# Routed tiles in pairs, three product buffers, a ring of twelve gathered tiles, and scatters in column halves

## The chip, the cores and the metric

The kernel runs on one core of a Trainium2 chip. The metric is device time in microseconds (us) of one execution. Engines are named as in the profile: PE (TensorE, with its weight loads apart as PEld), DVE (VectorE), ACT (ScalarE), POOL (GpSimd, which also issues the indirect DMAs) and SP (SyncE, which issues the plain ones). SBUF is the on-chip memory, PSUM the memory into which PE writes, in 8 banks of 512 fp32 columns for each of 128 partitions.

## The reference

The input is 64 sequences of 64 tokens with 256 columns, 4096 tokens. Each sequence has a category (0 to 15) and a language (0 to 3). Three steps run one after the other, the first two only feed the third:

```python
x = x + attn(x @ cond_weight[category] + cond_bias[category])   # 16 heads of 16, linear position bias
x = x @ A[language].T @ B[language].T + lang_embed[language]    # rank 16
def geglu(h): a, g = split(h, 2); return a * gelu(g)
ys = geglu(x @ Ws1 + bs1) @ Ws2 + bs2                           # shared expert, 512 hidden
w  = softmax over the two largest of (x @ Wr + br) / 1.5        # 2 of 12 experts per token
yr = sum_e w[:, e] * (geglu(x @ We1[e] + be1[e]) @ We2[e] + be2[e])   # 768 hidden each
out = residual stream + ys + yr
```

The experts of a token are known only on the chip. Each of the 4096 tokens has two, so there are 8192 pairs of a token and an expert. They are sorted by expert into tiles of 128 rows, each tile of one expert; rounded up for every expert this is at most 75 tiles, and the kernel always runs 75 (rows that belong to no token point at a zero row, and their results are added to spare rows behind the output).

## The kernel before

The first 412 us or so do attention, the low-rank step, the router and most of the shared expert; the change leaves them alone but for the stores. The routed stage that follows takes the rest. Its input rows are short: because the language step has rank 16, a token is kept as 69 numbers (64 low-rank ones, the language and a one; the router's gate stands in a 70th, rows are 72 wide) in `gated_rows` in HBM, and the first expert layer has been multiplied beforehand with the low-rank matrices (`w1m`, a 64-row matrix for every expert, and `w1b` for the biases and language rows).

One routed tile t goes through these steps. Tiles are numbered 0 to 74; s is t modulo the ring `RING` = 6, and buffers alternate by s modulo 2.

- POOL `load_rows` (L496): an indirect DMA gathers 128 rows of 288 bytes into `s_row[s]`, one of six buffers.
- ACT `widen` (L700, L702): two copies bring the rows into the form that can be transposed.
- PE `rows_transpose` (L1543, L1544): two transposes into PSUM bank 7. DVE `rowT_copy` (L1117, L1119) takes them out.
- The tile's expert weights are copied from `w1m` and `w1b` to a fixed place by `copy_first`, a third each by ACT, DVE and POOL (all on L270), and the bias rows by POOL (L511). Each such copy first loads the expert's number into a register (L269).
- PE `first_layer` (L1556, L1562): for each of three column blocks two bf16 matmuls for the biases and four for the rows, which the trace shows as eight fp32 records; two 64-row matmuls run beside each other. Output in banks 0 to 3, one set for all tiles.
- ACT `gelus` (L708), two halves; DVE `multiply` (L1127), two halves, into `actT_sb`, two buffers.
- PE `second_layer` (L1575): six matmuls of 256 columns, twelve records, into bank 4 or 5.
- DVE `gate_bias` (L1134) scales the expert's second bias row by the gate; `add_bias` (L1143) multiplies the product by the gate, adds it, and writes `y_sb`, one of three buffers.
- POOL `add_rows` (L504): an indirect DMA adds the 128 rows of 1024 bytes to the rows of the output. Two tiles can hold rows of one token, so a scatter waits (`d_add`) until the one before has landed.

The order on every engine is written by hand. PE runs first_layer(t+1), rows_transpose(t+2), second_layer(t). DVE runs rowT_copy(t+1), both halves of multiply(t), the weight copy for t+2, gate_bias(t), add_bias(t-1). POOL runs the copies for t+2, add_rows(t-1) and load_rows(t+5). Engines hand over through semaphores (`rowT_ps`, `rowT_sb`, `h_ps`, `g_ok`, `act_ok`, `y_ps`, `y_ok`), each of which is raised once or twice per tile.

Before the first scatter the residual plus shared result must stand in the output: SP `store_out` (L371) stores 32 tiles of it from `x2res`.

## Time and profile before

| | us |
|---|---|
| median of 3 runs | 805.79 (805.69 to 806.53) |
| profiled execution, its own time | 806.17 |
| its span, first to last instruction | 804.4 |
| granted TensorE clock, mean over the span | 0.996 |

The span is what the profile's rows cover; 1.8 us of the profiled execution lie outside it. Columns of a line of instruction groups: line, engine, operation, output <- inputs, count | busy time in us, mean ns of one | idle time of the engine before them, and who ended it. The first routed matmul starts at 434.4 us, the first scatter at 445.9, the last at 797.5. Matmuls are pipelined, so a row's length on PE is longer than the distance to the next; distances between starts tell the pace.

### The profile page before, as it was taken

The numbers are of one execution on the slowest core, as the hardware profiler recorded it, in microseconds if no ns is written. First come the engines' busy times: TensorE is split into PE (matmuls) and PEld (weight loads), VectorE is DVE, ScalarE is ACT, GpSimd is POOL, SyncE is SP. The second block draws the span as 40 slices with busy tenths as digits, with TensorE's granted clock in tenths as the row PEclk, the third lists the DMA queues.
The fourth block names the chain that finished last, engine by engine and source line by source line (L and its number), as shares of the span: only waits on it lengthen the run. The fifth ranks groups of instructions, "written<-read, shape, count | busy, mean of one in ns | idle before, by whom it ended". The sixth has DMA issues, their size and how long they took to land.

```text
span 804.4 us, 27682 instructions
## 1 busy us (share of the span) xinstructions
PE 783.6 (97%) x9379; PEld 658.2 (82%) x9380; DVE 575.9 (72%) x1350; ACT 294.3 (37%) x883; POOL 405.4 (50%) x511
## 2 busy tenths in 40 slices
PE   7999999999999999999999999999999999999994
PEld 6788888888888888777778888888888888888883
DVE  2999877777777777679884676666666666666661
ACT  1444444444444444542222333333333333333330
POOL 3133244444444444401012777777777777777762
PEclk9999999999999999999999999999999999999998
DMA  9553355555565554048734233223222322232222
GB/s 277 153 187 101 112 170 180 182 174 177 180 182 181 182 182 146 2 158 232 231 130 139 28 42 37 33 35 39 35 34 33 38 38 33 34 40 36 33 31 26
DMA packets 49325, 86.11 MB, mean 107 GB/s; under 512 B 7298, under 2 KB 27970, under 8 KB 49122
## 3 DMA queue, kind: packets, MB, share of 16 engines
q1 hardware_dynamic: 33778, 68.83, 27.2%
q0 software_dynamic: 13888, 15.13, 14.3%
q10 hardware_dynamic: 1584, 1.10, 0.5%
q8 instruction: 54, 0.88, 0.5%
q14 instruction: 21, 0.17, 0.1%
HBM read 68.48 MB, written 16.55 MB: 106 GB/s over the span
## 4 chain that ended last, share of the span: by engine, by line
PE 90%; DVE 5%; issue 2%; DMA 1%; SPq 0%; POOL 0%; ACT 0%; DVEq 0%
PE ps L1575 24%; PE ps L1562 13%; PE ps L1234 7%; PE ps L1473 6%; PE ps L1332 4%; PE ps L1556 4%; PE ps L1306 3%; PE ps L1250 3%; PE ps L1279 3%; PE ps L1462 3%; PE ps L1219 3%; PE ps L1543 2%; PE ps L1339 2%; PE ps L1292 2%; PE ps L1321 2%
## 5 line engine op out<-in xcount | busy, mean ns | idle before, releaser
L1575 PE MATMUL ps<-arena,stage 128*128 x900 | 206.6, 379 | 0.0
L1575 PEld LDWEIGHTS ps<-arena,stage 128*128 128x128 f32 x900 | 165.2, 190 | 19.5
L504 POOL DMA_INDIRECT out_dram<-stage,to_row x75 | 120.6, 1609 | 76.0 <-DVE stage L1143 71.3
L708 ACT ACTIVATE stage<-ps 128x384 f32<-128x384 f32 x150 | 65.4, 488 | 241.6 <-PE ps L1562 241.6
L1562 PE MATMUL ps<-token_rows,token_rows_T 64*128 64x128 f32 x1800 | 129.2, 272 | 0.0
L1562 PEld LDWEIGHTS ps<-token_rows,token_rows_T 64*128 64x128 f32 x1800 | 118.8, 188 | 1.7
L496 POOL DMA_INDIRECT token_rows<-gated_rows,from_row x75 | 75.1, 1001 | 61.6 <-DVE to_row L1022 38.9
L1117 DVE COPY token_rows<-ps 128x128 f32<-128x128 f32 x75 | 21.9, 292 | 111.8 <-PE ps L1544 111.8
L408 POOL TENSOR_TENSOR arena<-arena 128x256 f32<-128x256 f32 x32 | 23.4, 732 | 139.3 <-DVE arena L832 132.3
L1127 DVE TENSOR_TENSOR stage<-ps,stage 128x384 f32<-128x384 f32 x150 | 76.0, 549 | 1.8 <-ACT stage L708 1.8
L795 DVE TENSOR_REDUCE arena<-ps 128x8 f32<-128x512 f32 x64 | 43.9, 686 | 42.4 <-PE ps L1270 42.0
L1234 PE MATMUL ps<-arena 128*128 128x128 f32 x512 | 63.1, 276 | 0.9 <-ACT arena L565 0.8
L1556 PE MATMUL ps<-token_rows,token_rows_T 64*128 64x256 bf16 x450 | 62.1, 273 | 0.0
L1234 PEld LDWEIGHTS ps<-arena 128*128 128x128 f32 x512 | 59.7, 192 | 1.6 <-ACT arena L565 1.0
L1473 PE MATMUL ps<-ws,stage 128*128 128x256 f32 x256 | 59.1, 384 | 0.0
L578 ACT ACTIVATE arena<-arena 128x512 f32<-128x512 f32 x64 | 40.3, 630 | 50.0 <-DVE arena L797 49.7
L1473 PEld LDWEIGHTS ps<-ws,stage 128*128 128x128 f32 x256 | 47.4, 190 | 9.8 <-issue 4.0
L797 DVE TENSOR_TENSOR arena<-ps,arena 128x512 f32<-128x512 f32 x64 | 44.3, 691 | 2.2
L270 DVE COPY token_rows_T<-w_merged 128x256 f32 x75 | 44.7, 596 | 0.7 <-issue 0.7
L1119 DVE TENSOR_SCALAR token_rows<-ps,consts 128x128 bf16<-128x128 f32 x150 | 45.1, 343 | 0.0
L511 POOL COPY token_rows_T<-w_bias 128x384 bf16 x75 | 42.8, 570 | 0.9 <-issue 0.8
L590 ACT COPY arena<-arena 128x128 f32<-128x128 f32 x64 | 15.9, 295 | 73.4 <-DVE arena L817 73.4
(173 smaller groups left out, 1473.8 us busy)
## 6 DMA issues: line engine op xcount, KB each, us to landing
stage<-in_we_dram SPq DMA_DIRECT2D x36, 512.0 KB, 4.7
arena<-in_cond_w_dram SPq DMA_DIRECT2D x64, 256.0 KB, 2.8
arena<-in_we_dram SPq DMA_DIRECT2D x12, 768.0 KB, 6.0
arena<-in_x_both_dram SPq DMA_DIRECT2D x31, 256.0 KB, 2.7
arena<-in_L_cond_bias_dram SPq DMA_DIRECT2D x64, 64.0 KB, 2.9
out_dram<-arena SPq DMA_DIRECT2D x32, 128.0 KB, 2.7
be_bc<-in_be_rows_dram SPq DMA_DIRECT2D x13, 192.0 KB, 3.4
gated_rows<-token_rows POOLq DMA_DIRECT2D x2, 1152.0 KB, 11.6
```

The costliest lines, as they stand in the source:

```text
L270: copy(w1x[s % 2][:, j * CW:(j + 1) * CW], w1m[:, ds(e * (NJ * CW) + j * CW, CW)]).then_inc(w1x_ok[j], 1)
L496: pool.indirect_dma_start(s_row[s], None, gated_rows, bass.IndirectOffsetOnAxis(from_row[:, t:t + 1], 0)).then_inc(d_row[s], 16)
L504: pool.indirect_dma_start(out_rows, bass.IndirectOffsetOnAxis(to_row[:, t:t + 1], 0), y_sb[t % YR], None, compute_op=ALU.add).then_inc(d_a ...
L708: nc.scalar.activation(g_sb[hf].rearrange("p (j n) -> p j n", n=P), first_out[1][:, :, hf, :], ACT.Gelu).then_inc(g_ok, 1)
L797: V.tensor_tensor(probs[:, 512 * half:512 * half + 512].rearrange("p (g h k) -> p g h k", g=2, k=S), scores[:, banks], top.unsqueeze(3).to ...
L1119: last = V.tensor_scalar(s_langT[s % 2][:, hf * P:(hf + 1) * P], ps[:, 7, P:2 * P], col["half"][:, hf:hf + 1], None, ALU.mult)
L1127: V.tensor_tensor(actT_sb[s % 2][:, hf, :].rearrange("p (j n) -> p j n", n=P), first_out[0][:, :, hf, :], g_sb[hf].rearrange("p (j n) -> p ...
L1234: last = mm(ps[:, bank, at + m * P:at + (m + 1) * P], wm[w][:, k, m * P:(m + 1) * P], cT[:, k, :], start=(k == 0), stop=(k == KC - 1))
L1473: last = mm(ps[:, 4 + v, half * D:(half + 1) * D], sh_aT[half][:, k, v * P:(v + 1) * P], ws2[:, k, :], start=(k == 0), stop=(k == HS // P ...
L1556: mm(first_out[g][:, j].rearrange("p h n -> p (h n)"), w1bx[s % 2].bitcast(bf16)[64 * g:64 * g + 64, at], s_langT[s % 2][64 * g:64 * g + 6 ...
L1562: last = mm(first_out[g][:, j, hf, :], w1x[s % 2][64 * g:64 * g + 64, j * CW + hf * P:j * CW + (hf + 1) * P], s_rowT[s % 2][64 * g:64 * g ...
L1575: last = mm(ps[:, 4 + s % 2, 0:D], actT_sb[s % 2][:, hf, j * P:(j + 1) * P], arena[:, ds(e * E2 + (NJ * hf + j) * D, D)], start=(hf == 0 a ...
```

## The change

1. PSUM is divided anew. The first layer's output gets two sets, one for odd and one for even tiles, in banks 0 to 5 (each set is one and a half banks for each of its two parts, so both sets share two banks). The second layer's output goes to bank 6 for odd tiles and bank 7 for even ones; transposes share bank 7.
2. Tiles are handled in pairs (`two_tiles`): PE does the first layers of t and t+1, the transposes of t+2 and t+3, then the second layers of t-2 and t-1. DVE and ACT follow in an order of their own.
3. `actT_sb` gets a third buffer, in the space of `ws2`, which the shared expert has done with.
4. POOL makes no weight copies any more. DVE copies two thirds of `w1m`, ACT one third and the bias rows.
5. The ring of gathered rows has twelve places.
6. The output is two tensors of 128 columns. Each tile is scattered by two indirect DMAs of 128 rows of 512 bytes, each half waiting for the same half of the tile before; stores are two per tile as well, and the halves are joined on the host.
7. The last unit of the shared expert gets PSUM of its own (`last_shared`), so that the routed tiles can begin beside it.

On POOL, in the routed stage, this stands before for one tile (a scatter, a gather, two copies with their register loads) and then the next tile's scatter:

```order
L504 DMA out_dram<-stage,to_row 4224x256 [waits d_dummy,d_add,y_ok]
L496 DMA token_rows<-gated_rows,from_row 128x72
L269 TENSOR_LOAD expert_of [waits h_ps]
L269 ISA x2
L270 ISA
L270 COPY token_rows_T<-w_merged 128x256
L510 TENSOR_LOAD expert_of
L510 ISA x2
L511 ISA
L511 COPY token_rows_T<-w_bias 128x384
L504 DMA out_dram<-stage,to_row 4224x256 [waits d_dummy,d_add,y_ok]
```

and this now for two tiles (L513 is a half of a scatter, L503 a gather):

```order
L513 DMA out_dram<-stage,to_row 4224x128 [waits d_add0,d_dummy,y_ok]
L513 DMA out_dram<-stage,to_row 4224x128 [waits d_add1]
L503 DMA token_rows<-gated_rows,from_row 128x72 [waits y_ok] x2
L513 DMA out_dram<-stage,to_row 4224x128 [waits d_add0,d_dummy,y_ok]
L513 DMA out_dram<-stage,to_row 4224x128 [waits d_add1]
```

The copies are gone, the scatters have doubled, and both gathers of a pair stand between the scatters of an odd and an even tile, while those of an even and the next odd tile follow each other directly.

On VectorE, the loop before, one tile (waits of the copies of transposed rows, then multiply, weight copy, scaling, add):

```order
L1117 COPY token_rows<-ps 128x128 [waits rowT_ps]
L1119 TENSOR_SCALAR token_rows<-ps,consts 128x128 x2
L1124 ISA
L1127 TENSOR_TENSOR stage<-ps,stage 128x384 [waits g_ok]
L1124 REGISTER_ALU
L1127 TENSOR_TENSOR stage<-ps,stage 128x384 [waits g_ok]
L269 ISA
L269 TENSOR_LOAD expert_of
L269 ISA x2
L270 ISA
L270 COPY token_rows_T<-w_merged 128x256
```

and now the piece of the pair between the second copy of transposed rows and the add of the pair's first product (L275 copies weights, L1171 scales the bias):

```order
L1148 TENSOR_SCALAR token_rows<-ps,consts 128x128 x2
L274 ISA
L274 TENSOR_LOAD expert_of
L274 ISA x2
L275 ISA
L275 COPY token_rows_T<-w_merged 128x256
L274 TENSOR_LOAD expert_of
L274 ISA x2
L275 ISA
L275 COPY token_rows_T<-w_merged 128x256
L1168 TENSOR_LOAD expert_of
L1168 ISA x2
```

A second such scaling follows, then the add, and only behind it the multiply of the pair's second tile. Four instructions that each need a register load now stand in front of the add.

The core of the diff:

```diff
-RING = 6
+RING = 12
...
+        actT_sb.append(ws2[:, 0:NJ, :].rearrange("p k n -> p (k n)").rearrange("p (h n) -> p h n", h=2))
-        first_out = [ps[:, 2 * g:2 * g + 2, :].rearrange("p b n -> p (b n)")[:, 0:2 * HH].rearrange(
-            "p (j h n) -> p j h n", h=2, n=P) for g in range(2)]
+        hidden_ps = ps[:, 0:6, :].rearrange("p b n -> p (b n)").rearrange(
+            "p (g s j h n) -> p s g j h n", g=2, s=2, h=2, n=P)
+        def first_out(t, s):
+            return hidden_ps[:, 0 if s % 2 == 1 or isinstance(t, int) and t == 0 else 1]
+        last_shared = [ps[:, 6, 0:D], ps[:, 7, 0:D]]
...
             def store_out(n, d_out):
                 sp.wait_ge(comb_ok, n + 1)
-                sp.dma_start(out_rows[ds(n * P, P), :], x2res[:, ds(n * D, D)]).then_inc(d_out, 16)
+                for h in range(2):
+                    sp.dma_start(out_half[h][ds(n * P, P), :], x2res[:, ds(n * D + h * P, P)]).then_inc(d_out, 16)
...
             def add_rows(t, s):
                 pool.wait_ge(y_ok, t + 1)
-                if t > 0:
-                    pool.wait_ge(d_add, 16 * t)
-                pool.wait_ge(d_dummy, 16)
-                pool.indirect_dma_start(out_rows,
-                                        bass.IndirectOffsetOnAxis(to_row[:, t:t + 1], 0),
-                                        y_sb[t % YR], None, compute_op=ALU.add).then_inc(d_add, 16)
-
-            def copy_last(t):
-                copy_first(pool, nc.gpsimd.tensor_copy, t, t, 2)
-                e = pool.value_load(expert_of[0:1, ds(t, 1)], min_val=0, max_val=NE - 1)
-                nc.gpsimd.tensor_copy(w1bx[t % 2].bitcast(bf16), w1b[:, ds(e * (NJ * P), NJ * P)]).then_inc(w1bx_ok, 1)
+                pool.wait_ge(d_dummy, 32)
+                for h in range(2):
+                    part = slice(h * P, (h + 1) * P)
+                    if t > 0:
+                        pool.wait_ge(d_add[h], 16 * t)
+                    pool.indirect_dma_start(out_half[h],
+                                            bass.IndirectOffsetOnAxis(to_row[:, t:t + 1], 0),
+                                            y_sb[t % YR][:, part], None, compute_op=ALU.add).then_inc(d_add[h], 16)
...
+            def next_rows(t):
+                pool.wait_ge(y_ok, t + 1)
+                if t + RING < NS:
+                    load_rows(t + RING, t % RING)
+            for t in range(1, NS, 2):
+                if t > 1:
+                    add_rows(t - 2, (t - 2) % RING)
+                    next_rows(t - 2)
+                    next_rows(t - 1)
+                add_rows(t - 1, (t - 1) % RING)
+                if t == 1:
+                    next_rows(0)
+            for t in (NS - 2, NS - 1):
+                add_rows(t, t % RING)
...
+            def tile_weights(t, s):
+                copy_first(act, copy, t, s, 0)
+                e = act.value_load(expert_of[0:1, ds(t, 1)], min_val=0, max_val=NE - 1)
+                copy(w1bx[s % 2].bitcast(bf16), w1b[:, ds(e * (NJ * P), NJ * P)]).then_inc(w1bx_ok, 1)
+            def two_tiles(t, k, q):
+                for d in range(2):
+                    gelus(t + d, k + d, RING // 2 * q + (k + 1) // 2)
+                    if not (isinstance(t, int) and t + d + 2 >= NS):
+                        tile_weights(t + d + 2, k + d + 2)
+                for d in (4, 5):
+                    if not (isinstance(t, int) and t + d >= NS):
+                        widen(t + d, (k + d) % RING, 16 * q + 16 * ((k + d) // RING) + 16)
...
+            def multiply(t, s):
+                for hf in range(2):
+                    dve.wait_ge(g_ok, 2 * t + (hf + 1))
+                    if hf == 0 and isinstance(t, int) and t < 3:
+                        dve.wait_ge(shy_ps, NT - 2 if t == 0 else NT)
+                    elif hf == 0:
+                        dve.wait_ge(y_ps, t - 2)
+                    V.tensor_tensor(actT_sb[s % 3][:, hf, :].rearrange("p (j n) -> p j n", n=P),
+                                    first_out(t, s)[:, 0, :, hf, :], g_sb[hf].rearrange("p (j n) -> p j n", n=P),
+                                    ALU.mult).then_inc(act_ok, 1)
+            def tile_weights(t, s):
+                for j in (1, 2):
+                    copy_first(dve, V.tensor_copy, t, s, j)
...
             def add_bias(t, s):
+                bank = 6 if s % 2 == 1 or isinstance(t, int) and t == 0 else 7
                 dve.wait_ge(y_ps, t + 1)
                 dve.wait_ge(gb_ok, t + 1)
                 if not (isinstance(t, int) and t < YR):
...
+                    for h in range(2):
+                        dve.wait_ge(d_add[h], 16 * t - 16 * (YR - 1))
+                V.scalar_tensor_tensor(out=y_sb[s % YR], in0=ps[:, bank, 0:D],
                                        scalar=s_row[s][:, W_COL:W_COL + 1], in1=gated_be2[s % 2],
                                        op0=ALU.mult, op1=ALU.add).then_inc(y_ok, 1)
...
+            def two_tiles(t, k):
+                known = isinstance(t, int)
+                multiply(t, k)
+                if not (known and t + 2 >= NS):
+                    for d in (2, 3):
+                        rowT_copy(t + d, (k + d) % RING, t + 4)
+                    tile_weights(t + 2, k)
+                if not (known and t == 1):
+                    gate_bias(t - 2, (k - 2) % RING)
+                gate_bias(t - 1, (k - 1) % RING)
+                if not (known and t == 1):
+                    add_bias(t - 2, (k - 2) % RING)
+                multiply(t + 1, k + 1)
+                if not (known and t + 2 >= NS):
+                    tile_weights(t + 3, k + 1)
+                add_bias(t - 1, (k - 1) % RING)
...
                 last.then_inc(h_ps, 1)
...
+            def second_layer(t, s):
+                e = pe.value_load(expert_of[0:1, ds(t, 1)], min_val=0, max_val=NE - 1)
+                bank = 6 if s % 2 == 1 or isinstance(t, int) and t == 0 else 7
+                if not (isinstance(t, int) and t == 0):
+                    pe.wait_ge(y_ok, max(t - 1, 1) if isinstance(t, int) else t - 1)
+                if bank == 7:
+                    pe.wait_ge(rowT_sb, min(t + 5, NS) if isinstance(t, int) else t + 5)
                 for hf in range(2):
                     pe.wait_ge(act_ok, 2 * t + (hf + 1))
...
                     for j in range(NJ):
...
+                        last = mm(ps[:, bank, 0:D], actT_sb[s % 3][:, hf, j * P:(j + 1) * P],
                                   arena[:, ds(e * E2 + (NJ * hf + j) * D, D)], start=(hf == 0 and j == 0),
                                   stop=(hf == 1 and j == NJ - 1))
                 last.then_inc(y_ps, 1)
...
+            def two_tiles(t, k):
+                known = isinstance(t, int)
+                for d in (0, 1):
+                    first_layer(t + d, k + d)
+                for d in (2, 3):
+                    if not (known and t + d >= NS):
+                        rows_transpose(t + d, (k + d) % RING)
+                for d in (2, 1):
+                    if not (known and t < d):
+                        second_layer(t - d, (k - d) % RING)
```

## Rows read from the trace of the kernel before

**Rows 1.** The page: busy time, share of the span, instructions, by engine.

```profile
PE 783.6 (97%) x9379; PEld 658.2 (82%) x9380; DVE 575.9 (72%) x1350; ACT 294.3 (37%) x883; POOL 405.4 (50%) x511
```

**Rows 2.** Who waited for whom, 460 to 804: us, times, longest.

```profile
ACT stage L708 <- PE ps L1562: 223.0, 70, 3.9
...
POOL out_dram L504 <- DVE stage L1143: 69.2, 71, 3.6
```

**Rows 3.** PE in order of time: start, length, what; one tile.

```profile
600.70 0.38 PE L1575 MATMUL ps<-arena,stage 128*128 x1
601.01 0.28 PE L1556 MATMUL ps<-token_rows,token_rows_T 64*128 64x256 bf16 x2
...
602.78 0.33 PE L1543 MATMUL ps<-consts,token_rows 128*128 128x128 f32 x1
602.95 0.27 PE L1544 MATMUL ps<-consts,token_rows 128*128 128x128 f32 x1
603.06 2.76 PE L1575 MATMUL ps<-arena,stage 128*128 x12
...
605.75 0.28 PE L1556 MATMUL ps<-token_rows,token_rows_T 64*128 64x256 bf16 x2
```

**Rows 4.** VectorE in order of time, and the scatter behind it.

```profile
432.63 0.28 DVE L270 COPY token_rows_T<-w_merged 128x256 f32 x1
433.29 0.29 DVE L270 COPY token_rows_T<-w_merged 128x256 f32 x1 [0.37 <-issue]
...
603.26 0.29 DVE L1117 COPY token_rows<-ps 128x128 f32<-128x128 f32 x1 [1.55 <-PE ps L1544]
...
603.98 1.01 DVE L1127 TENSOR_TENSOR stage<-ps,stage 128x384 f32<-128x384 f32 x2
...
605.95 0.48 DVE L1143 SCALAR_TENSOR_TENSOR stage<-ps,token_rows,token_rows_T 128x256 f32<-128x256 f32 x1
...
606.72 1.61 POOL L504 DMA_INDIRECT out_dram<-stage,to_row  x1 [0.89 <-DVE stage L1143]
...
780.14 0.29 DVE L270 COPY token_rows_T<-w_merged 128x256 f32 x1
780.58 0.35 DVE L1134 TENSOR_SCALAR token_rows_T<-be_bc,token_rows 128x256 f32 x1
```

**Rows 5.** GpSimd: scatters and gathers (groups), and one gather behind a scatter.

```profile
L504 POOL DMA_INDIRECT out_dram<-stage,to_row x75 | 120.6, 1609 | 76.0 <-DVE stage L1143 71.3 <-issue 4.7
L496 POOL DMA_INDIRECT token_rows<-gated_rows,from_row x75 | 75.1, 1001 | 61.6 <-DVE to_row L1022 38.9 <-issue 22.7
...
447.78 1.01 POOL L496 DMA_INDIRECT token_rows<-gated_rows,from_row  x1 [0.31 <-issue]
```

**Rows 6.** GpSimd's two plain DMAs of 128 rows (288 and 1024 bytes).

```profile
L454 POOL DMA_DIRECT2D gated_rows<-be_bc x1 | 0.8, 761 | 0.0
L455 POOL DMA_DIRECT2D out_dram<-be_bc x1 | 0.6, 592 | 0.0
```

**Rows 7.** Scatters: median us to landing; the last two; their landings.

```profile
out_dram<-stage,to_row POOLq DMA_INDIRECT x75, 3.8
...
791.56 1.55 POOL L504 DMA_INDIRECT out_dram<-stage,to_row  x1 [3.00 <-DVE stage L1143]
...
797.53 1.55 POOL L504 DMA_INDIRECT out_dram<-stage,to_row  x1 [4.42 <-issue]
...
DMA to landing us min/median/max: 3.7/4.5/5.2
```

**Rows 8.** Start of the routed stage: tile 1 on PE, and POOL.

```profile
439.99 0.28 PE L1556 MATMUL ps<-token_rows,token_rows_T 64*128 64x256 bf16 x2
...
442.99 0.40 POOL L270 COPY token_rows_T<-w_merged 128x256 f32 x1 [15.44 <-DMA out_dram<-arena]
```

**Rows 9.** A gather and a VectorE copy that began during it.

```profile
623.52 1.00 POOL L496 DMA_INDIRECT token_rows<-gated_rows,from_row  x1 [0.31 <-issue]
...
623.86 0.76 DVE L270 COPY token_rows_T<-w_merged 128x256 f32 x1
```

More of the change, by code:

```diff
@@ L47, in adaln_attn_moe @@
     a = args
-    out_rows = out
     ctx = ExitStack()
@@ L535, in _ @@
+            for t in (NS - 2, NS - 1):
+                add_rows(t, t % RING)
+            for h in range(2):
+                pool.wait_ge(d_add[h], 16 * NS)
         @block.scalar
@@ L722, in _ @@
             act.wait_ge(shx_ok, TOK // U)
+            act.wait_ge(l_cut, 4 * (NE + 1))
             for t in range(2):
@@ L725, in _ @@
             for t in range(2):
-                copy_first(act, copy, t, t, 0)
+                tile_weights(t, t)
             shared_gelu(TOK // U - 1)
-            routed_tiles(0)
-            with act.Fori(1, NS // RING) as q:
-                routed_tiles(q)
-            routed_tiles(NS // RING, last=True)
+            widen(2, 2, 16)
+            gelus(0, 0)
+            tile_weights(2, 2)
+            for t in (3, 4):
+                widen(t, t, 16)
+            for k in range(1, RING, 2):
+                two_tiles(k, k, 0)
+            with act.Fori(1, NS // RING - 1) as q:
+                for k in range(1, RING, 2):
+                    two_tiles(RING * q + k, k, q)
+            for k in range(1, RING, 2):
+                two_tiles(NS - 3 - RING + k, k, NS // RING - 1)
+            two_tiles(NS - 2, 1, NS // RING)
         @block.vector
@@ L1163, in _ @@
             dve.wait_ge(r_done, 1)
             dve.wait_ge(shx_ok, TOK // U)
-            rowT_copy(0, 0)
+            rowT_copy(0, 0, 1)
             for t in range(2):
-                copy_first(dve, V.tensor_copy, t, t, 1)
+                tile_weights(t, t)
             for v in range(2):
                 combine(TOK // U - 2, v, 0)
+            for t in (1, 2):
+                rowT_copy(t, t, 3)
+            multiply(0, 0)
+            tile_weights(2, 2)
+            for v in range(2):
+                combine_last(v)
@@ L1170, in _ @@
             dve.wait_ge(d_be2, 16)
-            routed_tiles(0, first=True)
+            for k in range(1, RING, 2):
+                two_tiles(k, k)
             with dve.Fori(1, NS // RING) as q:
-                routed_tiles(q)
-            routed_tiles(NS // RING, last=True)
-            add_bias(NS - 1, (NS - 1) % RING)
+                for k in range(1, RING, 2):
+                    two_tiles(RING * q + k, k)
+            two_tiles(NS - 2, 1)
+            for t in (NS - 2, NS - 1):
+                gate_bias(t, t % RING)
@@ L1177, in _ @@
+            for t in (NS - 2, NS - 1):
+                add_bias(t, t % RING)
         @block.tensor
```

164 lines of the change are left out of this document (65 added, 99 removed).

## Prediction

> **What bounds the kernel now.** I read the page's busy table first, then who waited for whom over the routed stage (the last 364 us), then one routed tile in order of time on TensorE, VectorE and GpSimd, then the tail. The busy table has PE at 97% [rows 1], and the waits show ACT, DVE and POOL waiting for others while PE itself has no entry to speak of [rows 2]: PE sets the pace. One tile on PE [rows 3]: the first layer starts at 601.01 and the next one at 605.75, a period of 4.74. The second layer starts at 603.06 and its last matmul at 600.70 + 4.74 = 605.44, so eleven steps take 2.38, 0.216 each, twelve 2.60, and the next first layer is 0.09 late. I read that as the change of shape between 128 rows and pairs of 64, and give the same 0.09 to the other change, so the first layer's 601.01 to 602.78 is 1.68 + 0.09. The two transposes take 0.17 and 0.11. POOL is the second: per tile a gather of 1.00 and a scatter of 1.61, both pure issuing work, plus two copies of weights [rows 5]. It still waits for VectorE's result, 69.2 us in 71 times, 1.0 per tile [rows 2], so it has slack, but not much.
>
> **Pairs on PE.** Two first layers, four transposes, two second layers: 3.36 + 0.09 + (0.17 + 3 x 0.11) + 5.20 + 0.09 = 9.24 per pair, against 2 x 4.74 = 9.48. That removes 0.24 in each of 37 pairs, 8.9 us, if nothing else is late. The expert number that PE loads between the two second layers has twelve queued matmuls in front of it; I cost it nothing.
>
> **VectorE and ScalarE.** Counted from a pair's start at 0: the last transpose starts at 3.84, VectorE begins 0.31 later (602.95 to 603.26) at 4.15, copies both gathered rows at 0.72 each (603.26 to 603.98) until 5.59, then two weight copies and two bias scalings, each with an address loaded in front of it. From copy to copy that is 0.66 (432.63 to 433.29), from copy to scaling 0.44 (780.14 to 780.58) [rows 4]; with 0.66, 0.50, 0.50 and 0.35 the product is added at 7.60, done 8.08, and the two multiplies take 1.01 until 9.09. The next pair's first layer waits for the second of them. With a hand-over of 0.29, as from L1143's end (605.95 + 0.48) to the scatter at 606.72, that is 9.38, already a little past PE's 9.24. So even with POOL out of the picture the gain is 37 x 0.1 = 3.7 us rather than 8.9; I keep both ends. VectorE's extra copy (0.28 alone) is in this sum. ScalarE takes over the 128x384 bias copy. It waits for PE 223.0 us in 70 tiles [rows 2], 6.4 per pair, and two more small copies fit in there at anything up to 3 us each: nothing. The third product buffer and the doubled PSUM of the first layer take waits away from nobody who waits today.
>
> **GpSimd.** Here is the term that decides. Per pair it now issues four half scatters and two gathers in order, and nothing else. What does half a scatter cost? The trace has no scatter of 512-byte rows, so I bound it. The gather of 288-byte rows takes 1.00, the scatter of 1024-byte rows 1.61 [rows 5]; were it bytes, a half would lie at 1.19 by a line through the two. But two plain writes of 128 rows show the opposite of growth with bytes, 0.59 for 1024-byte rows and 0.76 for 288-byte rows [rows 6]. A half still has 128 row numbers and 128 additions. I take 1.61, with 1.00 as the lower end (and 0.8, half of it, as the extreme).
>
> The Trainium skill ("DMA: Bandwidth & Descriptors", Anatomy of one DMA, the gpsimd path) says the cost of such a DMA is about 2 us fixed plus its bytes over 436 GB/s, most of the fixed part being the receipt of the last write. By that rule 64 KB saved is an estimated 0.15 us of a transfer, so two halves cost nearly two wholes. It speaks of the whole transfer, not of the issuing; by rows 6 the trace agrees that bytes matter little.
>
> Behind each of these instructions POOL is free again only 0.31 later (447.78, "issue") [rows 5]. So the issuing alone is 4 x 1.61 + 2 x 1.00 + 6 x 0.31 = 10.30 per pair: more than PE's 9.24 and more than today's 9.48.
>
> There is a wait inside it too. A half may be issued only when the same half of the tile before has landed. Landing takes 3.8 from the issue's start in the median, and at the end of the kernel POOL's next scatter started 0.77 after the 5.2 it took there (791.56 + 5.2 = 796.76, start 797.53; of the last two landings I give the longer to tile 73, with the shorter the hand-over would be 2.3) [rows 7]. In POOL's order h0 of an even tile and h0 of the odd tile behind it have only one half scatter between them, 2 x 1.92 = 3.84, but need 3.8 + 0.77 = 4.57. Between odd and even the two gathers fill the time. So POOL's pair is 2 x 1.92 + 2 x 1.31 + 4.57 = 11.03. A half may land sooner than a whole, which brings it back towards 10.30; I take 11.03, since 3.8 already contains 1.61 of issuing and I leave that unchanged. With three y buffers VectorE's add waits for the scatter three tiles back, then PE for VectorE, so the whole pipeline settles at POOL's pace and PE sits idle for about 1.8 per pair.
>
> **The sum.** The first pair's first layers start where tile 1's starts now, at 439.99 [rows 8]; tile 0's second layer starts 3.36 + 0.59 later, its last matmul 2.38 after that, the add 0.51 on (605.44 to 605.95), the scatter 0.77 after the add (605.95 to 606.72) [rows 4]: 447.6. The stores of the shared part become two per tile; POOL waited for them until 442.99 [rows 8] and needs them 4.6 later than that, so nothing. From tile 0's scatter to tile 74's there are 37 pairs. The last gather is of row 74, issued behind tile 62, so 31 of them hold gathers, 31 x 11.03 = 341.9; in the last six POOL needs 2 x 4.57 = 9.14 and PE's 9.24 counts, 55.4. Then the second half starts 1.92 later, and from there to the end I take today's 804.4 - 797.5 = 6.8. Together 447.6 + 341.9 + 55.4 + 1.9 + 6.8 = 853.6, against the span of 804.4. Outside the span lie 806.2 - 804.4 = 1.8; the profiled execution is 0.4 over the median of the runs. Forecast: 853.6 + 1.8 - 0.4 = 855.
>
> **The rivals.**
> - *Half a scatter costs 1.0 or less.* For it: nothing in rows 6 is an indirect DMA, and the gather shows that 128 row numbers can be issued in 1.00. Then POOL needs 2 x 1.31 + 2 x 1.31 + (3.2 + 0.77) = 9.2 and VectorE's chain or PE sets 9.24 to 9.48: the gain of 37 x 0.1 to 0.24 comes through, and about 1.6 in the tail, since h0 lands earlier. Time about 800, between 795 and 805. This is the case on the other side. With s for a half, landing and issuing together make POOL's pair 3s + 6.2, which passes today's 9.48 at s = 1.09: there it decides.
> - *In between, 1.2 to 1.4*, as by bytes. With 1.3: 2 x 1.61 + 2.62 + (3.5 + 0.77) = 10.1, and 31 x 10.1 + 55.4 + 457.7 = 826 (457.7 are the 447.6, 1.9 and 6.8 of the sum, and 1.8 - 0.4).
> - *VectorE is held by POOL's issuing.* The weight copy that started at 623.86, while the gather of 623.52 ran, took 0.76 instead of 0.28 and ended 0.10 after the gather [rows 9]. So a copy between SBUF tiles waits until some 0.18 before the end of a POOL instruction. Today POOL's issuing meets at most one such copy per tile. After the change POOL issues nearly all the time, and four such VectorE instructions stand in the chain in front of the add. If two of them meet a half scatter for up to 1.43 each, the chain is 9.38 + 2.86 = 12.2 and leads (a copy met for less costs less): 31 x 12.2 + 55.4 + 457.7 = 891. Against it: in the chain's window POOL is mostly between its pairs of halves, waiting for landings.
> - *POOL is held by VectorE.* The Trainium skill ("SBUF — State Buffer", Who interferes with whom) says that an exclusive lock goes to whichever of the two starts first and blocks the other entirely. So far the trace shows one direction, VectorE waiting; the gathers stayed at 1.00. As a mechanism here: six VectorE instructions of 0.28 to 0.35 per pair, each delaying POOL by its length, make 11.03 + 1.9 = 12.9 and 31 x 12.9 + 55.4 + 457.7 = 913.
>
> **Chances.** Forecast (a half at 1.5 to 1.65, POOL's pace, 10.3 to 11.3 per pair, so 832 to 862) 0.50; VectorE held 0.16; POOL held 0.05; in between 0.12; a half at 1.0 or less 0.17, of which 0.14 come out faster by more than 0.2% and 0.03 within it. 0.2% (1.6 us) is about what runs of this kernel can tell. Faster 0.14, within 0.17 - 0.14 = 0.03, slower 0.83. The range of 803 to 888 leaves out most of the fast case and most of the last.
>
> **What would show it.** In the profile after: the mean of the scatter row (1.6 with x150 for me, 1.0 for the first rival); POOL's busy share over 80% in the routed slices; PE's busy share falling and PE or VectorE waiting for POOL or for a DMA; a period of 11 us per pair that drops to about 9.2 for the last six; VectorE's weight copies at 0.28 (forecast) or over 1 us (third rival); scatters longer than 1.61 (fourth). I am wrong if the half scatter's mean is under 1.1, or if POOL waits for VectorE every tile as it does now.

## The result and the profile after

The changed kernel takes 844.15 us in the median of four runs (841.85 to 845.8), the kernel before 805.9 on the same chip. The ratio is 1.0474, 95% interval 1.0461 to 1.0488: 38 us slower. The profiled execution took 841.85, with a span of 839.8. The forecast was 855, slower.

The page of the changed kernel: the busy table, the busy row of GpSimd in 40 slices, the scatters' group, the one of VectorE's additions (`add_bias`, from here on simply additions), and the scatters' issues to landing.

```profile
PE 783.3 (93%) x9379; PEld 663.3 (79%) x9380; DVE 571.3 (68%) x1425; ACT 330.5 (39%) x958; POOL 453.6 (54%) x437
...
POOL 3242244444444445010043777877778777878775
...
L513 POOL DMA_INDIRECT out_dram<-stage,to_row x150 | 237.8, 1585 | 79.2 <-issue 53.2
...
L1182 DVE SCALAR_TENSOR_TENSOR stage<-ps,token_rows,token_rows_T 128x256 f32<-128x256 f32 x75 | 36.2, 482 | 78.4 <-DMA out_dram<-stage,to_row 76.3
...
out_dram<-stage,to_row POOLq DMA_INDIRECT x150, 3.3
```

Half a scatter takes GpSimd 1585 ns, a whole one took 1609 [rows 5]. There are 150 now, so scatters take 237.8 us of it instead of 120.6. Landing, the time from the start of the issue to the semaphore event that tells of its end, fell only from 3.8 [rows 7] to 3.3.

Who waited for whom in the changed kernel from 460 us to the end (us, times, longest):

```profile
DVE stage L1182 <- DMA out_dram<-stage,to_row: 76.3, 51, 3.5
POOL out_dram L513 <- issue: 52.9, 137, 1.3
...
PEld ps L1621 <- DVE stage L1159: 19.1, 19, 1.3
...
PE ps L1621 <- DVE stage L1159: 11.6, 17, 0.9
```

In [rows 2] GpSimd waited for VectorE, 69.2 us. Now VectorE waits for scatters to land, 76.3 us, before it may write a product buffer again, and TensorE waits for VectorE. GpSimd's "issue" is 137 times the gap behind an indirect DMA, 0.3 us, or the rest of a landing.

GpSimd in order of time, one pair of the changed kernel and the start of the next:

```profile
627.32 1.56 POOL L513 DMA_INDIRECT out_dram<-stage,to_row  x1 [1.71 <-DMA out_dram<-stage,to_row]
629.18 1.56 POOL L513 DMA_INDIRECT out_dram<-stage,to_row  x1 [0.30 <-issue]
631.05 1.01 POOL L503 DMA_INDIRECT token_rows<-gated_rows,from_row  x1 [0.30 <-issue]
632.37 0.98 POOL L503 DMA_INDIRECT token_rows<-gated_rows,from_row  x1 [0.30 <-issue]
633.66 1.62 POOL L513 DMA_INDIRECT out_dram<-stage,to_row  x1 [0.30 <-issue]
635.59 1.57 POOL L513 DMA_INDIRECT out_dram<-stage,to_row  x1 [0.30 <-issue]
637.69 1.55 POOL L513 DMA_INDIRECT out_dram<-stage,to_row  x1 [0.53 <-issue]
```

I call the two halves of a tile's scatter h0 and h1. From pair to pair here 637.69 - 627.32 = 10.37, and five of its six intervals are one issue plus 0.3. The only longer wait, 0.53, stands before 637.69: h0 of the next tile, 4.03 after the h0 of 633.66. This wait is not always so short: before 627.32 it was 1.71. In the whole stretch with gathers, from 450.75 to 780.69 (the starts of tile 0's and tile 62's first halves), 31 pairs took 329.94, 10.64 each.

TensorE in windows of the changed kernel (PE busy is the first number behind the length):

```profile
446.00:520.00 74.00, 72.54 (x700) 64.05 (x699) 48.83 (x147) 33.37 (x102) 54.28 (x39) 1.00 0.29 31
520.00:780.00 260.00, 235.01 (x2177) 200.65 (x2177) 152.19 (x441) 99.69 (x293) 205.84 (x149) 1.00 0.32 33
780.00:822.00 42.00, 39.52 (x326) 34.03 (x322) 23.38 (x66) 12.70 (x36) 32.90 (x22) 1.00 0.35 33
```

It loses 25 us (260.00 - 235.01) from 520 to 780, at a granted clock of 1.00, so a lower clock has no part in it. In the first 74 us it loses little: the three product buffers let it run ahead.

### The profile page after: what moved, and what is told of

Read it like the earlier page. It is cut to its first block, busy times and chain, and to the rows that moved or that the text cites. A ratio compares the mean times of both kernels' runs of the same rounds, so it can differ in the third digit from the quotient of the medians.

```text
span 839.8 us, 27855 instructions
## 1 busy us (share of the span) xinstructions
PE 783.3 (93%) x9379; PEld 663.3 (79%) x9380; DVE 571.3 (68%) x1425; ACT 330.5 (39%) x958; POOL 453.6 (54%) x437
## 4 chain that ended last, share of the span: by engine, by line
PE 49%; POOL 28%; issue 11%; DVE 6%; DMA 5%; SPq 1%; DVEq 1%; ACT 0%; POOLq 0%
POOL out_dram L513 22%; PE ps L1290 6%; POOL token_rows L503 6%; PE ps L1531 5%; DMA out_dram<-stage,to_row 4%; PE ps L1388 4%; PE ps L1362 3%; PE ps L1306 3%; PE ps L1335 3%; PE ps L1518 3%; PE ps L1275 3%; PE ps L1644 2%; PE ps L1395 2%; PE ps L1348 2%; PE ps L1627 2%
## 5 line engine op out<-in xcount | busy, mean ns | idle before, releaser
L513 POOL DMA_INDIRECT out_dram<-stage,to_row x150 | 237.8, 1585 | 79.2 <-issue 53.2
L1644 PE MATMUL ps<-arena,stage 128*128 x600 | 137.4, 382 | 8.8 <-DVE token_rows L1148 5.8
L1644 PEld LDWEIGHTS ps<-arena,stage 128*128 128x128 f32 x600 | 111.6, 190 | 27.6 <-issue 13.6
L1627 PE MATMUL ps<-token_rows,token_rows_T 64*128 64x128 f32 x1800 | 127.2, 272 | 0.0
L503 POOL DMA_INDIRECT token_rows<-gated_rows,from_row x75 | 74.8, 997 | 63.2 <-DVE to_row L1050 40.6
L1182 DVE SCALAR_TENSOR_TENSOR stage<-ps,token_rows,token_rows_T 128x256 f32<-128x256 f32 x75 | 36.2, 482 | 78.4 <-DMA out_dram<-stage,to_row 76.3
L1644 PE MATMUL ps<-arena,ws 128*128 x300 | 69.8, 382 | 2.3 <-DVE stage L1159 1.8
L1159 DVE TENSOR_TENSOR stage<-ps,stage 128x384 f32<-128x384 f32 x100 | 50.8, 549 | 28.3 <-ACT stage L721 17.3
L1644 PEld LDWEIGHTS ps<-arena,ws 128*128 128x128 f32 x300 | 56.0, 190 | 11.7 <-issue 4.4
L275 DVE COPY token_rows_T<-w_merged 128x256 f32 x150 | 46.6, 331 | 8.9 <-issue 7.5
L1171 DVE TENSOR_SCALAR token_rows_T<-be_bc,token_rows 128x256 f32 x75 | 27.6, 368 | 31.1 <-issue 30.4
L1621 PEld LDWEIGHTS ps<-token_rows,token_rows_T 64*128 64x128 bf16 x450 | 22.8, 96 | 30.0 <-DVE stage L1159 19.1
```

What stands on the lines that cost most here:

```text
L275: copy(w1x[s % 2][:, j * CW:(j + 1) * CW], w1m[:, ds(e * (NJ * CW) + j * CW, CW)]).then_inc(w1x_ok[j], 1)
L503: pool.indirect_dma_start(s_row[s], None, gated_rows, bass.IndirectOffsetOnAxis(from_row[:, t:t + 1], 0)).then_inc(d_row[s], 16)
L513: pool.indirect_dma_start(out_half[h], bass.IndirectOffsetOnAxis(to_row[:, t:t + 1], 0), y_sb[t % YR][:, part], None, compute_op=ALU.add). ...
L1159: V.tensor_tensor(actT_sb[s % 3][:, hf, :].rearrange("p (j n) -> p j n", n=P), first_out(t, s)[:, 0, :, hf, :], g_sb[hf].rearrange("p (j n ...
L1621: mm(first_out(t, s)[:, g, j].rearrange("p h n -> p (h n)"), w1bx[s % 2].bitcast(bf16)[64 * g:64 * g + 64, at], s_langT[s % 2][64 * g:64 * ...
L1627: last = mm(first_out(t, s)[:, g, j, hf, :], w1x[s % 2][64 * g:64 * g + 64, j * CW + hf * P:j * CW + (hf + 1) * P], s_rowT[s % 2][64 * g:6 ...
```

## The experiments

### One scatter of whole rows

The pairs, the ring, the third product buffer and the new order are kept; rows are scattered whole into one output tensor, with the stores and waits that go with it.

```diff
-                for h in range(2):
-                    part = slice(h * P, (h + 1) * P)
-                    if t > 0:
-                        pool.wait_ge(d_add[h], 16 * t)
-                    pool.indirect_dma_start(out_half[h],
-                                            bass.IndirectOffsetOnAxis(to_row[:, t:t + 1], 0),
-                                            y_sb[t % YR][:, part], None, compute_op=ALU.add).then_inc(d_add[h], 16)
...
+                if t > 0:
+                    pool.wait_ge(d_add, 16 * t)
+                pool.indirect_dma_start(out_rows,
+                                        bass.IndirectOffsetOnAxis(to_row[:, t:t + 1], 0),
+                                        y_sb[t % YR], None, compute_op=ALU.add).then_inc(d_add, 16)
```

> The changed kernel with its pairs, its ring of twelve, its three product buffers and its order on every engine, but one scatter of whole rows into one output tensor again. My theory: the doubled scatters are the whole loss. GpSimd then issues 2 x 1.6 for scatters and 2 x 1.0 for gathers, with four gaps of 0.31 that is 6.4 us a pair, and the landing of one scatter before the next costs about 4.1 to 4.6 from scatter to scatter, so two of them take 9.1 at most; TensorE's 9.24 a pair is the bound again. From the first scatter at 450.8: 37 pairs x 9.3 to 9.5 and about 9 at the end give a span of 804 to 811 and a time of 806 to 813 by 37 full pairs; since the first ten pairs ran ahead of the scatters in the changed kernel, I take 798 to 812, thus no clear difference from 805.9. Rival A: pairs, ring and buffers cost by themselves (longer VectorE chain, later start): 825 or more. Rival B: the new order gains much and the halves hid it: below 790.

814.05 us, ratio to the kernel before 1.0099 (1.0082 to 1.0116). Of the 38 us the halves are 30, and 8 are left without them: 2 us above the range I expected, and well under rival A's 825. In the spans (812.3 against 804.4) 5.5 of it are the start, the first scatter at 451.33 instead of 445.8; 1.3 are the 74 steps to the last scatter, 353.0 against 351.7; 1.1 lie behind that. So the question is why the steps gained nothing. GpSimd in order of time, at two places:

```profile
568.51 1.63 POOL L509 DMA_INDIRECT out_dram<-stage,to_row  x1 [0.43 <-issue]
573.16 1.58 POOL L509 DMA_INDIRECT out_dram<-stage,to_row  x1 [3.02 <-DVE stage L1176]
575.04 1.02 POOL L501 DMA_INDIRECT token_rows<-gated_rows,from_row  x1 [0.31 <-issue]
576.36 0.97 POOL L501 DMA_INDIRECT token_rows<-gated_rows,from_row  x1 [0.30 <-issue]
577.88 1.62 POOL L509 DMA_INDIRECT out_dram<-stage,to_row  x1 [0.55 <-issue]
...
795.12 1.55 POOL L509 DMA_INDIRECT out_dram<-stage,to_row  x1 [2.99 <-DVE stage L1176]
799.75 1.55 POOL L509 DMA_INDIRECT out_dram<-stage,to_row  x1 [3.08 <-DMA out_dram<-stage,to_row]
804.30 1.55 POOL L509 DMA_INDIRECT out_dram<-stage,to_row  x1 [3.00 <-DMA out_dram<-stage,to_row]
```

From start to start it is 4.65, 4.72, 4.63, 4.55, whether gathers stand between or not: issue, landing, hand-over, next issue. The median of all 74 distances is 4.66; ten are 4.97 or more, and a chain with no slack never makes them good, so the mean is 4.77. The first two of the ten, 6.85 and 5.69, stand at the very start. Some rows name VectorE as the one that came last. Its additions of tiles 25 and 26, the two that the scatters of 573.16 and 577.88 carry, show otherwise:

```profile
569.77 0.48 DVE L1176 SCALAR_TENSOR_TENSOR stage<-ps,token_rows,token_rows_T 128x256 f32<-128x256 f32 x1
571.86 0.48 DVE L1176 SCALAR_TENSOR_TENSOR stage<-ps,token_rows,token_rows_T 128x256 f32<-128x256 f32 x1
```

They were done at 570.25 and 572.34, 2.9 and 5.5 before their scatters. In pairs the products come two at a time and queue up; in [rows 4] the scatter starts 0.29 behind its addition. In this run only the scatter of tile 1 was that close; every later one starts 1.65 or more behind the end of its addition. From tile 1 on the chain of scatters is the bound.

### One gather between every two tiles' scatters

The changed kernel with its halves; only GpSimd's order differs.

```diff
                 if t > 1:
                     add_rows(t - 2, (t - 2) % RING)
                     next_rows(t - 2)
-                    next_rows(t - 1)
                 add_rows(t - 1, (t - 1) % RING)
-                if t == 1:
-                    next_rows(0)
+                next_rows(t - 1)
```

> The changed kernel with GpSimd's order of a pair as scatters, gather, scatters, gather, in place of scatters, two gathers, scatters. My theory: 4.1 of the 10.64 us of a pair are the way from the first half of the even tile to the first half of the odd tile of the next pair, where the landing of 3.3 and 0.8 after it is waited for, though the issues between take 2 x 1.9. With a gather between, these issues take 5.2 and the landing is past: a pair takes 4 x 1.62 + 2 x 0.98 + 6 x 0.31 = 10.3, and 31 pairs save about 10 us: 832 to 836. Rival: issuing alone sets the pair and the landing is hidden anyway: 842 to 846. Rival: the gather waits for the odd tile's addition and GpSimd starts each pair later: above 846.

833.62 us, ratio 1.0344 (1.0327 to 1.0362): 10.5 us less than the changed kernel. GpSimd there in order of time, one pair and the start of the next:

```profile
599.01 1.60 POOL L513 DMA_INDIRECT out_dram<-stage,to_row  x1 [0.30 <-issue]
600.91 1.02 POOL L503 DMA_INDIRECT token_rows<-gated_rows,from_row  x1 [0.30 <-issue]
602.24 1.58 POOL L513 DMA_INDIRECT out_dram<-stage,to_row  x1 [0.30 <-issue]
604.12 1.56 POOL L513 DMA_INDIRECT out_dram<-stage,to_row  x1 [0.30 <-issue]
605.98 1.01 POOL L503 DMA_INDIRECT token_rows<-gated_rows,from_row  x1 [0.30 <-issue]
607.30 1.58 POOL L513 DMA_INDIRECT out_dram<-stage,to_row  x1 [0.30 <-issue]
609.18 1.58 POOL L513 DMA_INDIRECT out_dram<-stage,to_row  x1 [0.31 <-issue]
```

609.18 - 599.01 = 10.17 with nothing between the instructions but the 0.3: here GpSimd's issuing is the whole bound. From tile 2's first half to tile 62's, 30 pairs took 305.7 us there and 316.9 in the changed kernel, 10.19 and 10.56 each: 0.37 of a pair was the landing wait, the rest issuing. All 74 steps took 9.5 us less, and the first scatter started 1.4 later.

### The kernel before with halves

Single tiles, ring of six, the buffers of before, GpSimd's own weight copies; the scatter is edited the other way round from the first experiment, with the stores and waits that go with it.

> The kernel before, its order by single tiles, ring of six and two product buffers kept, with only the scatter in two column halves into two output tensors. My theory: GpSimd's own work is then the bound of every tile: two scatters 2 x 1.9, a gather 1.3, its copy of a weight block and the copy of the widened block about 1.0 with two register loads, in all 5.9 to 6.3 a tile against 4.74: 75 x 1.2 to 1.5 more, 890 to 920. That is worse than the changed kernel, so the move of GpSimd's copies to ScalarE saved what the halves cost in part. Rival: an issue costs by its bytes, a half costs half, and the time stays within 800 to 815.

884.04 us, ratio 1.0967 (1.0948 to 1.0985), 6 us under the expected range. GpSimd in order of time, one tile and the next scatter:

```profile
598.62 1.60 POOL L507 DMA_INDIRECT out_dram<-stage,to_row  x1 [0.16 <-DVE stage L1148]
600.52 1.56 POOL L507 DMA_INDIRECT out_dram<-stage,to_row  x1 [0.30 <-issue]
602.39 1.01 POOL L497 DMA_INDIRECT token_rows<-gated_rows,from_row  x1 [0.30 <-issue]
603.40 0.41 POOL L269 COPY token_rows_T<-w_merged 128x256 f32 x1
603.74 0.58 POOL L514 COPY token_rows_T<-w_bias 128x384 bf16 x1
604.49 1.60 POOL L507 DMA_INDIRECT out_dram<-stage,to_row  x1 [0.16 <-DVE stage L1148]
```

5.87 a tile, just under my 5.9 to 6.3; the last tiles, without gathers, are cheaper. The halves alone cost the old order 78 us; all the rest of the change together (the two copies moved to ScalarE and VectorE, pairs, ring, buffers) wins 40 of them back. The ring of twelve and the third product buffer were never taken away by themselves.

### No addition

The changed kernel, with scatters that overwrite rows: the kernel leaves out the addition to what the output holds, so its output is not the reference's. It serves to time the issue alone.

```diff
-                                            y_sb[t % YR][:, part], None, compute_op=ALU.add).then_inc(d_add[h], 16)
+                                            y_sb[t % YR][:, part], None).then_inc(d_add[h], 16)
```

> The changed kernel with scatters that write their rows in place of adding them: the addition to what the output holds is left out. It tells why a scatter takes 1.6 us of GpSimd and a gather 1.0. Theory: the addition makes the issue dearer; without it a half takes about 1.0, issuing takes 4 x 1.0 + 2 x 1.0 + 6 x 0.31 = 7.9 a pair, and TensorE's 9.24 or the landing decide: 795 to 812. Rival: the direction (rows written by index in place of read by index) costs 1.6 by itself: issue stays at 1.5 to 1.6 and the time at 838 to 846. A landing that is shorter without the addition would show as well, and takes off at most 0.8 a pair, 25 us.

801.46 us, ratio 0.9951 (0.9934 to 0.9967). The scatters and VectorE's additions there (ns min/median/max, first and last start), and the page's landing:

```profile
L513 POOL DMA_INDIRECT out_dram<-stage,to_row x150: 963/996/1103, 451.6 to 790.8; - x150
...
L1182 DVE SCALAR_TENSOR_TENSOR stage<-ps,token_rows,token_rows_T x75: 471/483/486, 450.2 to 787.4; 128x256 f32<-128x256 f32 x75
...
out_dram<-stage,to_row POOLq DMA_INDIRECT x150, 2.2
```

The 150 half scatters issue in 996 ns, as long as a gather, so it is the addition that costs 0.6 us of GpSimd per instruction and 1.1 us of landing, not the direction. TensorE is the bound again: from the first addition of VectorE to the last (337.2 us, 74 tiles) it is 4.56 a tile, 9.11 a pair. That mean takes in the end, where tiles come faster; from tile 2 to tile 62 it is 9.26 a pair, and 9.47 in the kernel before. My TensorE figures in the prediction, 9.24 and 9.48, were right.

### Weight copies by ScalarE, with whole scatters

Based on the first experiment; the tile's three weight blocks are copied by one instruction of ScalarE, and VectorE copies none.

```diff
-                copy_first(act, copy, t, s, 0)
                 e = act.value_load(expert_of[0:1, ds(t, 1)], min_val=0, max_val=NE - 1)
+                copy(w1x[s % 2], w1m[:, ds(e * (NJ * CW), NJ * CW)]).then_inc(w1x_ok[0], 1)
...
-            def tile_weights(t, s):
-                for j in (1, 2):
-                    copy_first(dve, V.tensor_copy, t, s, j)
```

> The kernel with pairs and whole scatters (814.05 us), and the copies of a tile's first-layer weights made by ScalarE in one 128x768 copy, where VectorE made two of the three blocks. It takes about 0.6 us a tile off VectorE, and with it the copies that meet GpSimd's issuing. My theory, from the whole scatters' starts: each scatter waits for the landing of the one before, 4.6 to 4.7 us from start to start whether gathers lie between or not, and VectorE is not what is late, so the time stays: 808 to 816. Rival: VectorE's chain of a pair, 9.4 against TensorE's 9.24, is what costs the pairs their gain: then 797 to 803, as where the addition was left out.

805.4 us, ratio 1.0002 (0.9989 to 1.0016). Neither theory gave that; mine was wrong. VectorE's additions and GpSimd's scatters here, and then in the first experiment (ns min/median/max, first and last start):

```profile
L1173 DVE SCALAR_TENSOR_TENSOR stage<-ps,token_rows,token_rows_T x75: 475/484/486, 446.2 to 785.1; 128x256 f32<-128x256 f32 x75
L509 POOL DMA_INDIRECT out_dram<-stage,to_row x75: 1552/1579/1697, 447.6 to 794.6; - x75
```

```profile
L1176 DVE SCALAR_TENSOR_TENSOR stage<-ps,token_rows,token_rows_T x75: 464/479/485, 449.9 to 794.5; 128x256 f32<-128x256 f32 x75
L509 POOL DMA_INDIRECT out_dram<-stage,to_row x75: 1552/1579/1734, 451.3 to 804.3; - x75
```

The first scatter starts 3.7 earlier: the first routed matmul comes 2.2 earlier (433.4 against 435.7), and VectorE's copies no longer stand before its first addition. Scatters follow each other in 4.69 instead of 4.77, 6 us over 74. So VectorE's copies cost this kernel the start. They did not make additions too late for their scatters, for behind tile 1 none was; 1.6 of the 6 us lie in the first two distances, and why the others are shorter (a median of 4.63 instead of 4.66, and fewer long ones) is open. Against the kernel before, the first scatter is still 1.8 later, the 74 steps take 347.0 and not 351.7, and 0.8 is lost at the end. This is read from one execution of each, and the profiled one here, 804.14, is 1.3 under its median. What remains is the landing chain: additions end at 785.1, the last scatter starts at 794.6, 9.5 behind.

### Only the left half scattered

The changed kernel without h1: the kernel leaves out the right half of the routed sum. The two waits for both halves are shortened in the same way.

```diff
-                for h in range(2):
+                for h in range(1):
                     part = slice(h * P, (h + 1) * P)
```

> The changed kernel with only the left column half scattered: one scatter of 512-byte rows a tile, the right half of the routed sum is left out. One issue of 1.6 a tile as with whole scatters, but a landing of 3.3 (start to start 4.1) in place of 3.8 (4.6). My theory: with whole scatters the way from start to start, 4.6 to 4.7, has taken TensorE's place, 4.62 a tile; with 4.1 TensorE sets the pace again: 799 to 804. Rival: the number of adding scatters or their gap to the gathers costs, whatever they land in: 811 to 816, as with whole scatters.

804.63 us, ratio 0.9994 (0.9985 to 1.0004): 0.6 over the upper edge of my range and 9.4 below whole scatters. The rival, 811 to 816, falls. The two groups there:

```profile
L1182 DVE SCALAR_TENSOR_TENSOR stage<-ps,token_rows,token_rows_T x75: 465/480/484, 449.3 to 788.9; 128x256 f32<-128x256 f32 x75
L513 POOL DMA_INDIRECT out_dram<-stage,to_row x75: 1552/1579/1643, 450.7 to 795.9; - x75
```

The issue is 1579 ns for 512 bytes a row and 1579 for 1024: between these two sizes bytes play no part in it. With the shorter landing the scatters no longer queue up: from tile 9 to tile 69 every second one starts 0.7 or less behind its addition, so the chain has slack and the additions decide again, every 4.59 on average against 4.66. Its first scatter still starts 3.1 later than in the kernel with ScalarE's copies, so it gains little on that one.

### Halves, a gather between, and ScalarE's copies

The second experiment (a gather between) with ScalarE's copies, the edit of the fifth.

> The changed kernel in two halves, with a gather between every two tiles' scatters (833.6 us), and ScalarE making all copies of first-layer weights in one 128x768 copy. Scatters took 1.62 to 1.85 where they met VectorE's copies and 1.55 alone. My theory: the four scatters of a pair stay and GpSimd's issuing sets the pair, so only these stretches go, 150 x 0.02 to 0.03: 828 to 832. Rival: the way over VectorE to the product buffers matters, and relief of VectorE shows more: 820 or less. Rival: ScalarE's longer copies delay its activations: above 835.

827.25 us, ratio 1.0277 (1.0259 to 1.0294), just under my range. Its first scatter starts at 448.2 where the second experiment's starts at 452.1, which is 4.0 of the 6.4; the scatters' median fell from 1569 to 1559 ns. From tile 2 to tile 62 a pair takes 10.15, in the second experiment 10.19. Again I had left out the start.

### The last seven tiles in halves

Based on ScalarE's copies with whole scatters; from tile `T0` = 68 on rows are halved by an index, so the output stays one tensor.

```diff
+                for h in range(2):
+                    if t > T0:
+                        pool.wait_ge(d_half[h], 16 * (t - T0))
+                    pool.indirect_dma_start(out_rows.rearrange("r (h n) -> (r h) n", h=2),
+                                            bass.IndirectOffsetOnAxis(to_half[h][:, t:t + 1], 0),
+                                            y_sb[t % YR][:, h * P:(h + 1) * P], None,
+                                            compute_op=ALU.add).then_inc(d_half[h], 16)
```

> Pairs, whole scatters and ScalarE's copies (805.4 us), but the last seven tiles, 68 to 74, scattered in column halves, into the same output tensor seen as twice as many rows of 128 columns. There VectorE's last addition was at 785.1 and the last scatter at 794.6, nine late, because whole scatters follow each other at 4.6 while TensorE delivers a tile in 4.58 and three buffers let it run ahead. Halves follow at about 4.0 where no gathers are left (the changed kernel's last twelve tiles). My theory: six steps x 0.6 less, 1.9 more for the second half of the last tile, and up to 0.5 for its shorter landing: 2 to 3 us less, 802 to 804. Rival: two halves into one tensor land no sooner, or their rows wait for each other in it: no gain or a loss, 805 to 810. Rival: the pace is TensorE's even at the end: 805 to 807.

806.86 us, ratio 1.0015 (1.0002 to 1.0028). No gain, and outside my 802 to 804. Its scatters at the end, first and last two:

```profile
770.77 1.56 POOL L520 DMA_INDIRECT out_dram<-stage,to_half  x1 [3.22 <-DVE stage L1193]
772.63 1.56 POOL L520 DMA_INDIRECT out_dram<-stage,to_half  x1 [0.30 <-issue]
...
795.10 1.55 POOL L520 DMA_INDIRECT out_dram<-stage,to_half  x1 [0.68 <-issue]
796.96 1.56 POOL L520 DMA_INDIRECT out_dram<-stage,to_half  x1 [0.30 <-issue]
```

The pace is as expected, 24.3 for six tiles where whole scatters took 27.5, and the halves land in 3.3 in the median, as with two tensors. So neither rival's mechanism holds, though the time lies in their ranges. But the second half and the longer way to the end give back 2.2 of the 3.2, and tile 68 started at 770.8 instead of 767.1: the whole scatters ahead of it followed each other in 4.75 on average, not 4.70. Both kernels vary by over 5 us from run to run, so whether the two extra tables or chance lengthened the chain is open. No version that does the whole work beats the kernel before.

## Why the prediction was right, and where its terms were off

- *A half costs a whole in issuing* (1.61 taken, 1.585 measured). Right, and the step that decided. The first rival (1.0 or less) and the one in between fall with it. That 512 or 1024 bytes a row make no difference to the issue is shown by the left-half kernel, and why 1.6 and not 1.0 by the kernel with no addition. So my lower bound, "the gather shows that 128 row numbers can be issued in 1.00", was a real bound for another operation.
- *GpSimd sets the pace, its issuing alone makes 10.30 a pair.* Right: 10.17 measured where nothing else waits.
- *The landing wait of 4.57 makes it 11.03.* The mechanism was right (the gather between removes the wait), the size was not. I left landing at 3.8; it is 3.3, and h0 to h0 without gathers between took mostly 4.0 to 4.2. That makes 2 x 1.89 + 2 x 1.31 + 4.1 = 10.5; 10.64 on average. This is the largest miss: 31 pairs took 329.94 and not 341.9, 12.0 less. By the Trainium skill ("DMA: Bandwidth & Descriptors", Anatomy of one DMA, the gpsimd path) the 64 KB saved are an estimated 0.15 of a transfer; the trace gives 0.5, so here the measurement decides.
- *The last six pairs at TensorE's 9.24, 55.4.* Wrong, 48.2. I had both engines in step there. But TensorE had run ahead by three product buffers, so GpSimd had work waiting: tile 62's first half started 10.9 behind its addition, tile 71's still 3.7. Without gathers GpSimd took its own 4.02 a tile, the landing of a half, 3.25, and the same 0.77 to the next issue as in [rows 7]. 7.2 less.
- *The first scatter at 447.6.* It came at 450.75. I counted tile 0 behind the pair's transposes, but not that VectorE makes its multiplies and copies for tiles ahead before it adds tile 0; where it makes no copies, that scatter starts at 447.6 (the fifth experiment). 3.15 more.
- *The tail of 6.8 behind the last half's start.* 9.06. GpSimd's wait for the last half ends 3.4 after its start, against 3.7 in the kernel before, so 2.6 more lie behind the landing. Nearly all of it is one instruction, GpSimd's drain at the end of the program (last rows of this section): 5.2 against 2.7. With h1 at 830.74 the terms are 450.75 + 329.94 + 48.2 + 1.86 + 9.06 = 839.8.
- *VectorE held by GpSimd's issuing, 12.2 a pair.* No. The longest of its weight copies (last rows of this section) is 0.62, not over 1. In the kernel before 69 of the 75 such copies took over 0.4, but 59 of these ran into GpSimd's own copies, which the change removes, and only ten ended with a gather as in [rows 9]. A half scatter holds them less than a gather did there: 41 copies started in its first 0.55 us, and 40 of them took 0.32 or less; the 26 that started 0.55 to 0.8 in ended 0.4 before it did and took 0.39 to 0.61.
- *GpSimd held by VectorE, 12.9 a pair.* No, if the same rows are read for the scatters: by at most 1.757 - 1.552 = 0.2 in one scatter, and a mean only 33 ns above the shortest. The Trainium skill ("SBUF — State Buffer", Who interferes with whom) has the rule that the first comer blocks the other entirely. The trace does not bear that out for a running issue: those 40 copies went through inside one at close to their usual 0.28. In the other direction it decides nothing at this size.
- *What the pairs are worth without the halves: 3.7 to 8.9 gained.* Wrong in sign: 8 lost, 5.5 of them at the start. TensorE did gain: 9.26 a pair in the kernel with no addition, 9.47 before (VectorE's additions, tiles 2 to 62). But a whole scatter needs 4.6 to the next, 9.2 to 9.3 a pair, and that was hidden only under the slower single tiles. The 3.8 + 0.77 = 4.57 stood in my own working for halves; I never put it beside TensorE's 4.62 for wholes. Of the later start, VectorE's copies are 3.7 (the fifth experiment); the other 1.8 are open.

Of the misses, 12.0 and 7.2 were too much and 3.15 and 2.3 too little, so in part they cancel: the sum gave 853.6 for a span of 839.8.

The whole difference, 839.8 - 804.4 = 35.4, goes: 4.9 later at the first scatter (445.85 before), 26.4 in 74 steps (378.1 against 351.7), 1.9 for the second half, 2.2 behind it.

The weight copies of VectorE, the scatters and the drain of the changed kernel, then the drain of the kernel before (ns min/median/max, first and last start):

```profile
L275 DVE COPY token_rows_T<-w_merged x150: 273/288/617, 432.0 to 806.6; 128x256 f32 x150
L513 POOL DMA_INDIRECT out_dram<-stage,to_row x150: 1552/1564/1757, 450.7 to 830.7; - x150
L50 POOLq DRAIN  x1: 5217/5217/5217, 834.3 to 834.3; - x1
```

```profile
L51 POOLq DRAIN  x1: 2683/2683/2683, 801.4 to 801.4; - x1
```

## What to carry to other kernels

Count the issuing engine's time per indirect DMA by instructions and by what they do, not by bytes: cutting a transfer in two to shorten its landing pays only where the engine that issues has that time to spare. When scatters must follow each other, compare issue, landing and hand-over from start to start with the bound engine's step before speeding that engine up: here 4.6 lay hidden under 4.7. And where buffers let one engine run ahead of another, the work that waits between them is worked off at the slower one's own pace, so in the last tiles that engine's steps alone count, and not the larger of the two.

## What the hardware showed that I had not expected

- An adding scatter costs GpSimd 1.55 to 1.6 us to issue, a plain one 1.0, a gather 1.0, each of 128 rows; landing is 3.3 with the addition and 2.2 without for 512-byte rows, 3.8 for 1024-byte rows.
- Behind the last landing GpSimd drains before the program ends, and this took 2.7 us in the kernel before, 3.8 with whole scatters in pairs, 3.9 with halves in single tiles, 5.2 in the changed kernel and 5.7 with no addition. The number of indirect DMAs (150, 150, 225, 225, 225) doesn't settle it, and what does is open.
- Whether VectorE's copy of 0.28 us is held by GpSimd's issuing depends on when it starts. In the first 0.55 us of a half scatter 40 of 41 took 0.32 or less; from 0.55 to 0.8 all 26 ended 0.4 before the scatter's end, and took up to 0.61.
